# Where the value products of the second self attention stand: beside the last projection of layer one, or between the first row maxima of the attention itself

## What is computed

```
# end of layer one
x = (a * gelu(gate)) @ ff_w2 + ff_b2 + x
# start of layer two
h = layernorm(x, ln1_w, ln1_b)
qkv = h @ qkv_w + qkv_b                       # q, k, v: 16 heads of 16 each
attn = softmax(causal(q @ k.T * 16 ** -0.5))  # 1024 x 1024 for each batch and head
sa = attn @ v
```

## Time and profile before

| what | value |
|---|---|
| median of 3 runs | 1816.7 us (1816.31 to 1817.88) |
| the profiled execution | 1816.95 us, span 1815.2 us |
| PE, DVE, ACT, POOL busy | 91%, 63%, 59%, 53% of the span |
| mean granted TensorE clock | 0.977 of full speed |
| pf0 on PE, first product to last v product | from 1159.99 to 1241.68 us |
| prologue on PE, first maximum to first score | from 1242.88 to 1275.53 us |

### The profile page before, as it was taken

The page is one execution under the profiler, slowest core; times in us unless marked ns, Lnnn a source line. Parts: engine busy times, 40 slices in busy tenths (PEclk is TensorE's granted clock), DMA queues, the critical chain, the costliest instruction groups (busy, mean ns, idle before and its releaser), DMA issues. The chain is left out here.

```text
span 1815.2 us, 28598 instructions
## 1 busy us (share of the span) xinstructions
PE 1657.3 (91%) x9572; PEld 1025.1 (56%) x9572; DVE 1149.9 (63%) x2009; ACT 1067.1 (59%) x1407; POOL 959.6 (53%) x734
## 2 busy tenths in 40 slices
PE   5889999999999999988999889997898988898799
PEld 3334444444444444376666778885444436565579
DVE  4456777776777777385777753346778754776513
ACT  3436888888888888844554533311576763444452
POOL 1236888888888888951222630201334443466405
PEclk9999999999999999999999999997899999999899
DMA  2001211101110111030000010102333321000101
GB/s 91 18 24 36 68 41 48 41 35 41 38 61 35 41 35 36 24 105 27 1 1 1 13 33 24 30 13 49 91 72 96 81 63 42 9 1 1 35 16 47
DMA packets 54161, 70.82 MB, mean 39 GB/s; under 512 B 18160, under 2 KB 41868, under 8 KB 54063
## 3 DMA queue, kind: packets, MB, share of 16 engines
q1 hardware_dynamic: 54063, 69.54, 13.7%
HBM read 41.72 MB, written 2.37 MB: 24 GB/s over the span
## 5 line engine op out<-in xcount | busy, mean ns | idle before, releaser
L1412 POOL TENSOR_TENSOR x<-x,sa_p_buf 128x1024 f32<-128x1024 f32 x190 | 452.2, 2380 | 109.6 <-ACT sa_p_buf L1233 97.2
L1325 DVE TENSOR_REDUCE sa_mx<-sa_front 128x1 f32<-128x512 f32 x512 | 327.5, 681 | 109.1 <-PE sa_front L1126 107.7
L1233 ACT ACTIVATE sa_p_buf<-sa_score 128x1024 f32<-128x1024 f32 x256 | 249.2, 1024 | 115.9 <-PE sa_score L1164 115.9
L1179 PE MATMUL sa_out<-sa_p_buf,sa_v_buf 128*64 128x512 f32 x1024 | 246.2, 602 | 0.0
L607 ACT ACTIVATE sa_p_buf<-sa_score 128x1024 f32<-128x1024 f32 (+1 forms) x160 | 140.6, 943 | 75.0 <-PE sa_score L555 74.9
L402 DVE TENSOR_REDUCE sa_mx<-sa_front 128x1 f32<-128x512 f32 (+1 forms) x224 | 136.5, 651 | 31.4 <-PE sa_front L316 28.0
L2005 POOL TENSOR_TENSOR x<-x,bias_out 128x1024 f32<-128x1024 f32 x24 | 59.6, 2496 | 166.3 <-POOLq L2335 143.3
L1872 POOL TENSOR_TENSOR ca_probs<-ca_s_sb,ca_inv 128x616 f32<-128x616 f32 x64 | 77.9, 1218 | 120.8 <-DVE ca_inv L1787 120.8
L1179 PEld LDWEIGHTS sa_out<-sa_p_buf,sa_v_buf 128*64 128x64 f32 x1024 | 64.9, 136 | 126.9 <-issue 99.1
L1126 PE MATMUL sa_front<-sa_k_hi,sa_q_hi 64*128 64x512 f32 x512 | 116.7, 452 | 19.1 <-DVE sa_mx L1325 15.6
L1243 ACT ACTIVATE sa_score<-sa_m_all 128x1024 f32<-128x1024 f32 x128 | 130.8, 1033 | 1.0 <-DMA sa_m_all<-sa_m_line 0.6
(11 more groups left out here) (241 smaller groups left out, 3482.1 us busy)
## 6 DMA issues: line engine op xcount, KB each, us to landing
sa_v_buf<-o SPq DMA_DIRECT2D x16, 512.0 KB, 5.1
sa_m_all<-sa_m_line SPq DMA_DIRECT2D x16, 512.0 KB, 3.7
x<-sa_m_line SPq DMA_DIRECT2D x16, 512.0 KB, 4.4
x<-in_x SPq DMA_DIRECT2D x8, 512.0 KB, 6.7
sa_q_stack<-sa_hi SPq DMA_DIRECT2D x32, 128.0 KB, 2.6
sa_k_stack<-sa_hi SPq DMA_DIRECT2D x32, 128.0 KB, 2.6
sa_recip<-sa_den_out SPq DMA_DIRECT2D x32, 128.0 KB, 2.7
ff_w<-in_L_xattn_ff_w SPq DMA_DIRECT2D x16, 128.0 KB, 2.2
```

The costliest lines, as they stand in the source:

```text
L1179: mm = pe.matmul(out_ps[64 * j:64 * j + 64, :], v_buf[:, b, kt, 64 * j:64 * j + 64], p_buf[:, s % NPB, j, :], start=(kt == 0), stop=(kt == ...
L1233: nc.scalar.activation(p_buf[:, s % NPB], score_ps[s % len(score_ps)][:], ACT.Exp, scale=SCALE).then_inc(exp_done, G)
L1325: dve.tensor_reduce(mx[:, b, j, qt, half:half + 1], front_ps[bank(item, j)][:], AX.X, ALU.max).then_inc(drained, 1)
L1412: nc.gpsimd.tensor_tensor(acc[:, h], prev, cur, ALU.add).then_inc(added, 1)
```

## The change

The eight v items leave the slots of pf0. Five of them stand in `late` after every fourth maximum of item 0 (behind maxima 4, 8, 12, 16 and 20), and the last three stand between item 0's t and the first maximum of item 1. Nothing else changes: the same matmuls, the same DVE sums, the same banks for everything from the first maximum of item 1 on, no DMA more or less.

```
@@ -136,8 +136,13 @@
     early = [[] for _ in range(SLOTS)]
     for n in range(TT // GROUP):
         b, part = divmod(n, NPROJ)
-        early[n + 2] += [(b, ("p", part)), (0, ("v", n))]
-    late = [(0, m) for m in maxima] + [(0, ("t",))] + [(1, m) for m in maxima[:EARLY]]
+        early[n + 2].append((b, ("p", part)))
+    late = []
+    for n, m in enumerate(maxima):
+        late.append((0, m))
+        if n % 4 == 3:
+            late.append((0, ("v", n // 4)))
+    late += [(0, ("t",)), (0, ("v", 5)), (0, ("v", 6)), (0, ("v", 7))] + [(1, m) for m in maxima[:EARLY]]
     assert sum(item[0] == "v" for slot in early + [late] for _, item in slot) == 2 * NPROJ
```

## The result

The changed kernel is slower: 1828.3 us as the median of 7 runs (1822.6 to 1830.8), against 1816.7 us (1814.9 to 1822.5) for the kernel before on the same chips. The ratio is 1.0047 with a 95% interval of 1.0031 to 1.0063. In a second series the changed kernel's median was 1825.4 us against 1818.7, ratio 1.0041 (1.0027 to 1.0055). In microseconds both ratios are 7.5 to 8.5 us. The forecast was 1818.9 us, with 0.52 for a change too small to tell and 0.38 for slower; 1816.7 x 1.0047 is 1825.2 us, at the upper end of the range of 1812.5 to 1825.5, and the first series' median itself lies above it.

What follows compares the result with a forecast made beforehand. PE was taken to bound pf0, DVE the prologue up to t. Costs of 8.5 + 1.3 + 5.3 - 0.8 = 14.3 us minus 12.1 gained gave +2.2 us, forecast 1818.9 us, range 1812.5 to 1825.5.

Steps and rivals of the forecast that it cites:

- What bounds each stage: pf0 bound by PE; prologue by DVE's reductions up to t, then by PE and DVE in turn; transfers bound neither.
- Rivals 3 and 4: pf0 not getting shorter, about 1831 us, chance 0.03; delay behind t absorbed before the first score, 1814.4 us, chance 0.05.
- a first maximum later than 1231.5 us: Start of the prologue: listed as a sign that the forecast is wrong; the first maximum was expected near 1230.8 us.
- What pf0 gives back: In pf0: six slots save 1.73 us each, 10.4 us, and the tail 1.7 us; together 12.1 us.
- v0 to v3: Prologue, behind every fourth maximum of item 0: 2.5 us for v0 and 2.0 us for each other, 8.5 us paid.
- the low price: Prologue: cost of one value product among item 0's maxima at half clock (1.2 GHz), 2.5 us.
- the upper bound, 10.0 us: Prologue: cost of the first four moved products if all run at half clock, 10.0 us and not 8.5.
- rival 2: Prologue: low clock nearly throughout, 21.7 us paid against 12.1 gained, +9.6 us, 1826.3 us; chance 0.17.
- v4, t and v5 to v7: End of item 0 in the prologue: v4 pays 1.3 us, the three products behind t pay 5.3 us as the clock rises.
- The gain of item 1's maxima from the full clock: Prologue, behind the last products: first two or three maxima of item 1 at 1.35 us, not 1.64; 0.8 us back.
- The sum: Both stages: 14.3 us paid in the prologue minus 12.1 us gained in pf0, +2.2 us.

Runs made afterwards that it cites:

- three: Kernel before with only the last three value products moved, between t and item 1's maxima; the first five stay in pf0; ratio 1.0020.
- after_again: The changed kernel unaltered, run again for a second series and profile; ratio 1.0041 against the kernel before.
- five: Kernel before with only the first five value products moved, behind every fourth maximum; the last three stay in pf0; ratio 1.0026.
- filled_one: Changed kernel plus one matmul nobody reads behind each of the 15 maxima of item 0 followed by another maximum; ratio 1.0019 against the kernel before.
- kept_filled: Kernel before with v6 kept in pf0, other seven products behind maxima 1, 3, ... 13, plus 14 unread matmuls behind later maxima and t; ratio 0.9990.

## Why the prediction was right or wrong

**What bounds each stage: right.** pf0 was bound by PE, no transfer took over as the bound, and the first score starts behind the last maximum without idle time, now as before. Rivals 3 and 4 are out: pf0 gave back its microseconds, and `three` shows that nothing absorbs the delay behind t. The prediction's sign of a first maximum later than 1231.5 us did show (1236.73), but through the late start of pf0, not through pf0's length.

**What pf0 gives back: right.** Forecast 12.1 us; 12.0 in `after_again`, 11.2 in the first profile. The missing 0.9 us is a thing that I had not on the list: with v6 gone, PE idles 1.25 us ahead of the last transposes, besides the 0.90 us behind them that it idled before, and in one of the two executions the clock fell there already, so that the last q, k product took 2.01 us and not 1.13.

**v0 to v3: the step that failed.** The term was 8.5 us and measured 13.05 us: 2.99 for v0 (first to fifth maximum 7.23 us, against 4.24 before) and 10.06 for v1 to v3. Two things were in it. I discounted v1 to v3 from 2.5 to 2.0 us, in the hope that the clock would be up for some: 1.5 us. In `five` it was so in part, in both profiles of the changed kernel hardly. The other 3.05 us are the low price itself, 2.5 us where 3.0 to 3.35 were paid. At half clock a product takes 3.71 us from start to start and not 2 x 1.73 = 3.46; between maxima it takes 1.93 and not 1.73 even at full clock. And DVE's pace was not 1.14 us throughout, since some of the maxima have fewer columns (ten of them took 11.0 us before). With that the upper bound, 10.0 us, was no bound. Of the rivals, 2 described v0 to v3 best. Its argument from the trace was weaker than it said: the 37 us at 0.50 hold t, the first scores and a q, k product too, and maxima of item 0 alone only up to t at 1266.50, 21.5 us. By the Trainium skill, "TensorE: Matmul & The Clock Gate", section "HAM oscillation — how this bites in real kernels", a loop whose waits outlast its matmul work starts each round at half clock. With no discount at all, as rival 2 read that rule, the sum would have been +3.7 us, nearer than +2.2. The trace agrees for v1 to v3, which take 3.71 us each at 0.50; but between the first five products PE's waits were at most 1.35 us, shorter than a product, and the clock did rise in between, so the page's case is not quite this one.

**v4, t and v5 to v7: right.** 1.3 us forecast for v4; from maximum 17 to t it measured 0.95. The three behind t: 5.3 forecast, 5.08 measured, at full clock, with the rise at the end of v4, at t. The gain of item 1's maxima from the full clock: 0.8 forecast, 1.26 measured.

**The sum.** 13.05 + 0.95 + 5.08 - 1.26 = 17.8 us paid, 11.2 to 12.0 us gained: 5.8 to 6.7 us slower in the two stages, where I had 14.3 - 12.1 = +2.2. The timed ratios say 7.5 to 8.5 us. The 1 to 2 us between are not explained by the moved products: the stretch behind the loop is 1.9 us longer in both profiles of the changed kernel than in the one of the kernel before, and whether that one is short by chance stays open. That the time still lies in the range is owed to the range's width, which reached towards rival 2, and not to the term for v0 to v3.

## What to carry to other kernels

Before work is moved from a stage where TensorE is dense into one where it waits, read the granted clock of both stages: here matmuls of 1.73 us became 3.71 us, and idle time on TensorE was filled at half the rate. If such work is to fill gaps, put it close together and in the gaps from the start on: the same eight products cost 17.8 us at every fourth maximum and behind t, and 8.8 us at every second. And leave in the dense stage what stands where the engine waits anyway. It may also bring the clock further into the next stage: in the four profiles with a value product in slot 8 of pf0 the clock fell 0.2 to 4.2 us behind the first maximum, in the nine without between 3.8 us ahead of it and 0.4 us behind it. No run tests this by itself.

## What was unexpected of the hardware

- TensorE's granted clock fell while the engine was in use at short turns: maxima over 33 rows, one each 1.13 us (0.50 us of PE at full clock, 0.80 at half), stayed at 0.50 for 18 us before, and where they stood alone at 1.00 it fell again in every profile. With one 128-row matmul of 0.63 us between them it was 1.00 for 29 us (`filled_one`, 1240 to 1269); in `kept_filled` it fell at about 1264 us in spite of such filling.
- A value product takes 1.73 us among its like and 1.93 us between maxima, half a product 1.06 and not 0.87 us, at the same clock. The places differ in the shape of the neighbours, over 33 rows and over 128; that this is the cause is argued, not shown.
- The clock moves in places that nothing in the program singles out: the loop took 231.7 to 239.7 us in profiles of kernels whose loop is the same, and the cross attention of layer one, the same in all, differs by 4 us between the profiles of before and after. With times alone, 5 us can't be placed; by stages, 50.5 us repeats to 0.1.
